# Attention by pairs of head pairs: shared rounds on TensorE, wider VectorE and ScalarE operations, later output statistics

## The chip, the cores and the metric

One core of a Trainium2 chip runs the whole program. The metric is the device time of one execution in microseconds. The tensors are float32 unless a line says otherwise.

## The reference

Two layers on 2048 tokens (8 sequences of 256) of width 256. Layer 0 is two mixtures of experts (stages A and B below), layer 1 is attention (C) and a mixture of 16 experts with two chosen per token (D):

```python
x = x + _L0_ffn_ref(_L0_cond_ref(x, cond_64, ...), ...)
x = x + _L1_ffn_ref(_L1_cond_ref(x, fside_16xSxS_0, mask_BxS_bk0, ...), ...)
```

The attention has 16 heads of 64, one shared key and value head, a null key and value, a bias per head (256 x 256), a mask per sequence, and a causal limit. Its input rows and its output rows are layer-normalized. The output feeds the routing of stage D.

## The kernel before

The program is written by hand: each engine has its own list of instructions, and semaphores join them. Stages A and B come first, then attention (`pe_attention`, `act_attention`, `dve_attention`, `pool_attention`, `sp_attention`), then D's expert matmuls. The change is in attention, some 275 us of the program.

Attention goes through 8 batches (sequences) b, and in each through 8 pairs of heads j; p = 8b + j numbers the 64 pairs. Every engine's loop has the same steps p, and works in each on different pairs:

- **GpSimd** (`pool_batch`): `pool_bm` makes the sum of mask and bias for pair p + 2, one instruction per head (L2306). Between these: the combination of stage B's results for the next batch (`pool_pairs`, L2320, L2324), the powers for both normalizations (`pool_row_rstd`, `pool_out_rstd`), the dispatch of routed rows (L2387, from batch 3 on), and in step 7 of batches 1 to 7, behind its second sum, a wait for `z_step`, after which `pool_z` and `pool_z_again` multiply and copy the last batch's output (L2366, L2374, L2375).
- **TensorE** (`pe_batch`): step p issues scores of pair p + 1 (`pe_scores`, two heads side by side in 64 rows each, L1609), the sums over values of pair p - 4 (`pe_sum`, 64 columns each, L1622), the queries of pair p + 3 (`pe_queries`, L1595) and the output products of pair p - 5 (`pe_out`, L1633). Beside them stand the turned rows, keys and values of the next batch (`pe_rows`, `pe_kv`, `pe_v_turn`) and the route of stage D for an earlier batch (`pe_z_turn`, `pe_z_logits`, `pe_z_counts`). Scores have two banks, by j: pair p waits until VectorE has read both heads of pair p - 2.
- **VectorE** (`dve_batch`): step p does, in this order, the block transpose of pair p's head 1 (`dve_blocks`, L2011), the scores of pair p + 1's head 1 (`dve_scores`, L1986: adds the mask sum and finds the row minimum), the output product with the reciprocals for pair p - 4 (`dve_o`, L2020), the block transpose of head 0, the reciprocals (L1993, L2000), in odd steps parts of the route search (`dve_dispatch`), and the scores of pair p + 1's head 0. `dve_scores_wait` waits for TensorE's scores and for both mask sums of the pair. Step 1 also has the statistics of the next batch's input, step 5 the raw output of the last batch (`dve_out_raw`, L2029), its statistics (L2033, L2038) and its variance (L2043).
- **ScalarE** (`act_batch`): step p does the exponentials of pair p + 1's two heads (`act_exp`, L1849, two pieces each), and between them the copy and scaling of the queries (`act_queries`, L1843) and in step 7 the normalization of the last batch's output (`act_out`, L1817), whose end is `z_step`.
- **SP's queue** (`sp_attention`): the transposed blocks of pair p are stored to DRAM (`sp_store_blocks`, L2484, 512 KB) and read back with partitions and rows exchanged (`sp_load_blocks`, L2495); the load of pair p - 1 is issued behind the store of pair p. Two block buffers stand in front of the stores, four behind the loads. Weights of stage D are loaded between them.

The head order is `ORDER = (1, 0)` and `LAG = 4`, so "first head" below is head 1.

## Time and profile before

| | us |
|---|---|
| median of 3 runs (781.17 to 783.06) | 781.69 |
| the profiled execution, its own time | 780.06 |
| its span, first to last instruction | 778.2 |
| busy in the span: TensorE / weight loads | 700.5 / 544.4 |
| busy: VectorE / ScalarE / GpSimd | 471.2 / 395.0 / 430.8 |

The granted clock of TensorE is 0.956 of full speed over the span, and 1.00 in the whole of attention. TensorE's busy time is modelled, because matmuls overlap; the start times of its instructions are not. Attention's first scores start at 361.3 us, its last output products at 635.7. A wait is put down to whatever ended last by the trace.

### The profile page before, as it was taken

How to read it: one execution, taken by the hardware profiler on the slowest of the kernel's cores; microseconds unless marked ns; L12 is line 12 of the kernel's file. 1: busy time of each engine (PE TensorE's matmuls, PEld its weight loads, DVE VectorE, ACT ScalarE, POOL GpSimd, SP SyncE). 2: the span in 40 equal slices, each digit the busy share in tenths (PEclk: the TensorE clock that was granted, in tenths of full speed). 3: DMA queues.
4: the chain of work that ended last, by engine and by line, in shares of the span. 5: the costliest groups of instructions: out<-in, count | busy, mean ns of one | idle time of the engine just before them, and what ended most of it. 6: DMA issues, size and time to landing. Idle time of an engine off the chain costs nothing. (4 is left out here: it accounts for less than half of the span.)

```text
span 778.2 us, 15602 instructions
## 1 busy us (share of the span) xinstructions
PE 700.5 (90%) x4389; PEld 544.4 (70%) x4390; DVE 471.2 (61%) x1730; ACT 395.0 (51%) x1100; POOL 430.8 (55%) x540
## 2 busy tenths in 40 slices
PE   8878998675899999998799999899999989998986
PEld 5457995455699999986566666566666654887865
DVE  1722457267444445424888888899998945354546
ACT  4444651124344444424767657576766625765611
POOL 1075604560555685243876877898896654255550
PEclk9897999795699999999999999999999999999999
DMA  9834534345377777541899999888888773455428
GB/s 324 315 95 117 156 106 132 102 132 207 103 228 228 219 219 203 158 148 58 305 312 343 317 351 327 297 295 270 306 266 298 267 282 106 123 148 151 132 80 320
DMA packets 120813, 166.22 MB, mean 214 GB/s; under 512 B 29984, under 2 KB 97056, under 8 KB 119840
## 3 DMA queue, kind: packets, MB, share of 16 engines
q1 hardware_dynamic: 103632, 127.65, 49.3%
q0 software_dynamic: 10944, 30.03, 12.5%
q10 hardware_dynamic: 6160, 7.64, 3.0%
q8 instruction: 34, 0.56, 0.3%
q14 instruction: 43, 0.35, 0.1%
HBM read 100.07 MB, written 65.21 MB: 212 GB/s over the span
## 5 line engine op out<-in xcount | busy, mean ns | idle before, releaser
L1849 ACT ACTIVATE work<-work 128x129 f32<-128x129 f32 (+1 forms) x256 | 114.4, 448 | 73.7 <-DVE work L1986 72.6
L2011 DVE STREAM_TRANSPOSE region_bd<-work 128x384 f32<-128x384 f32 x128 | 73.1, 571 | 13.4 <-DMA c_blocks<-region_bd 9.3
L1430 POOL DMA_INDIRECT d_pairs<-work,home x47 | 47.6, 1012 | 52.5 <-DVE home_f L1180 35.3
L1595 PE MATMUL psY<-work,region_ac 128*128 128x256 f32 x256 | 70.0, 396 | 3.8 <-ACT work L1843 3.8
L2306 POOL TENSOR_TENSOR work<-region_bd,region_ac 128x386 f32<-128x386 f32 x64 | 59.6, 939 | 19.1 <-DVE work L1986 11.1
L1419 POOL DMA_INDIRECT b_pairs<-work,home x39 | 38.1, 976 | 56.7 <-DVE work L1124 54.6
L2306 POOL TENSOR_TENSOR work<-work,region_ac 128x386 f32<-128x386 f32 x64 | 59.6, 943 | 17.3 <-DVE work L1986 9.3
L1411 POOL DMA_INDIRECT work<-in_x,inv x39 | 37.2, 953 | 56.0 <-DVE inv L1337 36.0
L1633 PE MATMUL psM<-region_ac,work 128*128 128x256 f32 x256 | 66.9, 384 | 0.0
L1082 ACT ACTIVATE work<-work 128x512 f32<-128x512 f32 x39 | 24.6, 630 | 80.5 <-issue 46.9
L1622 PE MATMUL psL<-region_bd,work 128*64 128x256 f32 (+1 forms) x512 | 55.8, 338 | 7.2 <-DVE work L2020 3.9
L902 PE MATMUL psH<-work,region_bd 128*128 128x128 f32 x472 | 59.6, 281 | 1.0 <-issue 1.0
L902 PEld LDWEIGHTS psH<-work,region_bd 128*128 128x128 f32 x472 | 57.0, 197 | 2.0 <-issue 1.9
L1622 PEld LDWEIGHTS psL<-region_bd,work 128*64 128x64 f32 x512 | 31.6, 136 | 38.4 <-issue 23.6
L1547 POOL DMA_INDIRECT work<-a_slots,slot_u x32 | 31.3, 978 | 45.8 <-DMA a_slots<-work 27.0
L1411 POOL DMA_INDIRECT work<-y_scratch,inv x39 | 37.7, 968 | 32.9 <-DVE inv L1337 21.3
L1595 PEld LDWEIGHTS psY<-work,region_ac 128*128 128x128 f32 x256 | 44.7, 189 | 14.0 <-ACT work L1843 5.7
L1633 PEld LDWEIGHTS psM<-region_ac,work 128*128 128x128 f32 x256 | 47.1, 190 | 8.5 <-issue 2.8
L1986 DVE CUSTOM_DVE_ANT_0 work<-psH,work 128x129 f32<-128x129 f32 (+1 forms) x128 | 39.6, 346 | 13.7 <-issue 8.6
L1849 ACT ACTIVATION_READ_ACCUMULATOR work<-work 128x1 f32 x256 | 47.9, 187 | 0.0
L963 PEld LDWEIGHTS psH<-work,acc 128*128 128x128 f32 x320 | 41.0, 201 | 0.9
L2387 POOL DMA_INDIRECT d_rows<-region_bd x32 | 32.2, 1008 | 16.2 <-DMA d_rows<-region_bd 6.9
(392 smaller groups left out, 1649.5 us busy)
## 6 DMA issues: line engine op xcount, KB each, us to landing
c_blocks<-region_bd SPq DMA_DIRECT2D x64, 512.0 KB
region_bd<-c_blocks SPq DMA_DIRECT2D x64, 512.0 KB
work<-d_rows SPq DMA_DIRECT2D x47, 132.0 KB
a_slots<-work SPq DMA_DIRECT2D x19, 256.0 KB
b_turned<-work SPq DMA_DIRECT2D x35, 128.0 KB
work<-b_turned SPq DMA_DIRECT2D x35, 128.0 KB
region_bd<-in_b_w SPq DMA_DIRECT2D x1, 3072.0 KB, 21.5
region_ac<-in_fside SPq DMA_DIRECT2D x12, 256.0 KB
```

Of the source, the lines that this page charges most:

```text
L902: last = pe.matmul(pair_h[p % DEEP][:, t % PAIR, j, :], f.w_in(j, k, t), xT[:, p % DEEP, t % PAIR, k, :], start=(k == 0), stop=(k == KD - 1))
L963: last = pe.matmul(ffn_h[u % RING][:, j * P:(j + 1) * P], f.w_in(j, k, u % RING), b_xT[:, u % RING, :, k, :], start=(k == 0), stop=(k == K ...
L1411: pool.indirect_dma_start(out=slot_rows(f, t), out_offset=None, in_=st.src, in_offset=bass.IndirectOffsetOnAxis(ap=inv[:, t:t + 1], axis=0 ...
L1419: pool.indirect_dma_start(out=st.pair_dram, out_offset=bass.IndirectOffsetOnAxis(ap=home[:, t:t + 1], axis=0), in_=ys[:, t % RING, :], in_ ...
L1430: pool.indirect_dma_start(out=st.pair_dram, out_offset=bass.IndirectOffsetOnAxis(ap=home[:, t:t + 1], axis=0), in_=d_ys[:, t % ROWS, :], i ...
L1595: last = pe.matmul(psY[:, 0:SEQ], c_wq[:, c, j * P:(j + 1) * P], c_xnT[:, odd, c, :], start=(c == 0), stop=(c == KD - 1))
L1622: last = pe.matmul(psL[DH * o:DH * o + DH, queries].rearrange("p (i a q) -> p i a q", a=4, q=32), c_v[:, b % 2, n, :], weights[:, o, block ...
L1633: last = pe.matmul(psM[:, i * DIM:(i + 1) * DIM], c_oT[:, p % 3, i * P:(i + 1) * P], c_wo[:, j, :], start=(j == 0 and i == 0), stop=(j == ...
L1849: nc.scalar.activation(c_p[:, j % 2, o, a:z], c_sc[:, o, a:z], ACT.Exp, scale=-1.0, bias=c_min[:, o, i:i + 1], accum_out=c_sum[:, j % 2, o ...
L1986: last = nc.vector.tensor_tensor_reduce(c_sc[:, o, a:z], psS[j % 2][:, o, a:z], c_bm[:, 2 * (j % 2) + o, a:z], 1.0, -LOWEST, ALU.add, ALU. ...
L2011: nc.vector.transpose(out=c_x1[:, p % 2, :, (QT + 1) * o:(QT + 1) * (o + 1), :].rearrange("p b i q -> p i b q"), in_=c_p[:, j % 2, o, 1:1 ...
L2306: pool.tensor_tensor(c_bm[:, 2 * (j % 2) + o, :], c_mp[b % 2], c_bias[:, 2 * j + o, :], ALU.subtract).then_inc(C.bm_ready, 1)
```

## The change

- **TensorE** works on two pairs at a time, in four groups a batch. The group of a = 8b + 2k issues the scores of pairs a + 2 and a + 3, the sums of a - 4 and a - 3, the queries of a + 4 and a + 5, and the output products of a - 6 and a - 5. In the third group (k = 2) the output products stand before the queries, else behind them. Two pairs' sums share one PSUM bank, and two pairs' queries another.
- **VectorE** makes the output product of two pairs in one instruction (512 columns) in even steps, for pairs p - 6 and p - 5, ahead of the scores. It no longer computes the two variances. The raw output stays in step 5 but moves behind the second head's scores, the statistics go to step 6 (the last batch: 7), and a part of the route search goes from step 5 to step 3.
- **ScalarE** scales two pairs' queries at once, at the start of even steps. The normalization `act_out` moves behind the second head's exponentials of step 7. Rows, keys and values of the next batch move ahead of a second head's exponentials.
- **GpSimd** adds the epsilon for both variances (two small instructions a batch), and `pool_out_rstd` stands between the two sums of step 7, not behind those of step 6.
- **Blocks**: four buffers in front of the stores instead of two; the new ones lie where experts 8 to 11 of `d_w13` go. The load of pair p - 2 is issued behind the store of pair p. Eight experts' weights are loaded in batch 1, and eight behind attention; before, it was twelve and four.

The core of the diff:

```diff
@@ pe_batch
-                if not (last and j == NPAIR - 1):
-                    pe_scores(pe, p + 1, (j + 1) % NPAIR, b + (j + 1) // NPAIR)
-                if s >= 0:
-                    pe_sum(pe, s, s % NPAIR, s // NPAIR)
...
+            for k in range(NPAIR // 2):
+                a = NPAIR * b + 2 * k
+                x = a - LAG
+                for p in (a + 2, a + 3):
+                    if p < pairs:
+                        pe_scores(pe, p, p % NPAIR, p // NPAIR)
+                for s in (x, x + 1):
+                    if s >= 0:
+                        pe_sum(pe, s, s % NPAIR, s // NPAIR)
+                if k == 2:
+                    pe_outs(pe, x - 2)
...
+                for p in (a + 4, a + 5):
+                    if p < pairs:
+                        pe_queries(pe, p, p % NPAIR, p // NPAIR % 2, p // NPAIR)
...
+                if k != 2:
+                    pe_outs(pe, x - 2)
@@ pe_attention, the end
-            for j in range(NPAIR - LAG, NPAIR):
-                pe_sum(pe, pairs - NPAIR + j, j, BATCH - 1)
-                pe_out(pe, pairs - NPAIR + j - 1, j - 1, BATCH - 1)
+            for j in range(NPAIR - LAG, NPAIR, 2):
+                for i in (j, j + 1):
+                    pe_sum(pe, first + i, i, BATCH - 1)
+                pe_outs(pe, first + j - 2)
...
-            pe_out(pe, pairs - 1, NPAIR - 1, BATCH - 1)
+            pe_outs(pe, first + NPAIR - 2)
@@ act_batch
                 if more:
                     act_exp(act, p + 1, j + 1, ORDER[0])
...
-                if not (last and j + 3 >= NPAIR):
-                    act_queries(act, p + 3, j + 3)
-                if j == 7 and not first and not last:
-                    act_out(act, b - 1)
...
                 if more:
                     act_exp(act, p + 1, j + 1, ORDER[1])
+                if j == 7 and not first and not last:
+                    act_out(act, b - 1)
@@ dve_blocks, dve_o
-            if p >= 2 and n == 0:
-                wait_dma(dve, C.blocks_stored, 0, p - 2)
+            if p >= 4 and n == 0:
+                wait_dma(dve, C.blocks_stored, 0, p - 4)
...
-            dve.wait_ge(C.pv_mm, p + 1)
+            dve.wait_ge(C.pv_mm, p + 2)
             wait_dma(dve, C.blocks_loaded, 0, p)
+            wait_dma(dve, C.blocks_loaded, 0, p + 1)
@@ dve_batch
                 dve_blocks(dve, p, j, ORDER[0])
                 if j == 0 and not first:
                     dve_v(dve, b)
+                if j % 2 == 0 and p >= LAG + 2:
+                    dve_o(dve, p - LAG - 2)
                 if more:
                     dve_scores_wait(dve, p + 1)
                     dve_scores(dve, p + 1, j + 1, ORDER[0])
-                if s >= 0:
-                    dve_o(dve, s, s % NPAIR)
...
-                if j == 5 and not first:
-                    dve_out_raw(dve, b - 1)
+                if j == 6 and not first and not last:
+                    dve_out_stats(dve, b - 1)
+                    dve.wait_ge(C.out_step, 4 * b - 2)
+                    dve_out_moments(dve, b - 1)
                 dve_dispatch(dve, b, j, last)
                 if more:
                     dve_scores(dve, p + 1, j + 1, ORDER[1])
...
+                if j == 5 and not first:
+                    dve_out_raw(dve, b - 1)
                     dve.wait_ge(C.out_raw, 2 * b)
@@ pool_batch
-                    if (j, n) == ((7, 0) if last else (6, 1)) and not first:
+                    if (j, n) == (7, 0) and not first:
                         pool_out_rstd(pool, b - 1)
@@ sp_attention
-            for p in range(pairs):
-                sp_store_blocks(sp, p)
-                if p >= 1:
-                    sp_load_blocks(sp, p - 1)
+            for a in range(0, pairs, 2):
+                for p in (a, a + 1):
+                    sp_store_blocks(sp, p)
+                    if a >= 2:
+                        sp_load_blocks(sp, p - 2)
```

How it moves instructions, at three places. **ScalarE, pair step 7 of a batch and the start of the next** (L1849 before and L1881 after are the exponentials, two pieces a head; L1843 and L1871 the queries; L1817 and L1840 the normalization). Before:

```order
L1849 ACTIVATE work<-work 128x129
L1849 ACTIVATE work<-work 128x257
L1843 ACTIVATE work<-psY 128x256
L1817 ACTIVATE acc<-acc,out_shift,out_rstd 128x256 x2
L1849 ACTIVATE work<-work 128x129
L1849 ACTIVATE work<-work 128x257
L1849 ACTIVATE work<-work 128x129
L1849 ACTIVATE work<-work 128x257
L1843 ACTIVATE work<-psY 128x256
```

After:

```order
L1881 ACTIVATE work<-work 128x129
L1881 ACTIVATE work<-work 128x257
L1881 ACTIVATE work<-work 128x129
L1881 ACTIVATE work<-work 128x257
L1840 ACTIVATE acc<-acc,out_shift,out_rstd 128x256 x2
L1871 ACTIVATE work<-psY 128x512
L1881 ACTIVATE work<-work 128x129
L1881 ACTIVATE work<-work 128x257
```

The normalization stood behind one head of its step and now stands behind both, with the double query operation behind it.

**TensorE, third group of a batch** (L1609 and L1614 are scores, L1622 and L1628 sums, L1633 and L1639 output products, L1595 and L1600 queries, L1650 and L1662 keys and values). Before, its step 5:

```order
L1609 MATMUL psH<-region_bd,work 128x129 x2
L1609 MATMUL psH<-region_bd,work 128x257 x2
L1622 MATMUL psL<-region_bd,work 64x256 x2
L1622 MATMUL psL<-region_bd,work 64x128 x2
L1650 MATMUL psX<-work,region_ac 128x256 x2
L1595 MATMUL psY<-work,region_ac 128x256 x2
L1609 MATMUL psHT<-region_bd,work 128x129 x2
L1609 MATMUL psHT<-region_bd,work 128x257 x2
```

After:

```order
L1639 MATMUL psM<-region_ac,work 128x256 x4
L1662 MATMUL psX<-work,region_ac 128x256 x2
L1614 MATMUL psH<-region_bd,work 128x129 x2
L1614 MATMUL psH<-region_bd,work 128x257 x2
L1614 MATMUL psHT<-region_bd,work 128x129 x2
L1614 MATMUL psHT<-region_bd,work 128x257 x2
L1628 MATMUL psL<-region_bd,work 64x2x128 x2
L1628 MATMUL psL<-region_bd,work 64x128 x2
L1628 MATMUL psL<-region_bd,work 64x2x128 x2
L1628 MATMUL psL<-region_bd,work 64x128 x2
L1639 MATMUL psM<-region_ac,work 128x256 x4
L1600 MATMUL psY<-work,region_ac 128x256 x4
```

Keys and values now end the group ahead, and the products that complete the last batch (first L1639 behind the sums) stand behind two pairs' scores and sums.

**GpSimd, pair step 7** (L2306 and L2328 are mask sums, L2366 and L2394 z). Before:

```order
L2348 TENSOR_TENSOR out_rstd<-out_rstd,minus_half 128x2
L2349 TENSOR_SCALAR out_shift<-out_mv 128x2
L2351 TENSOR_TENSOR out_shift<-out_shift,out_rstd 128x2
L2306 TENSOR_TENSOR work<-work,region_ac 128x386 x2
L2366 TENSOR_TENSOR region_bd<-acc,g_out 128x256 x2
```

After:

```order
L2328 TENSOR_TENSOR work<-region_bd,region_ac 128x386
L2374 TENSOR_SCALAR out_rstd<-out_mv 128x2
L2376 TENSOR_TENSOR out_rstd<-out_rstd,minus_half 128x2
L2377 TENSOR_SCALAR out_shift<-out_mv 128x2
L2379 TENSOR_TENSOR out_shift<-out_shift,out_rstd 128x2
L2328 TENSOR_TENSOR work<-region_bd,region_ac 128x386
L2394 TENSOR_TENSOR region_bd<-acc,g_out 128x256 x2
```

The powers moved between the two sums of step 7 and gained the addition in front; z still stands behind the second sum.

## Rows read from the trace of the kernel before

**Rows 1.** Busy time by stretch: batches 1 and 5
```profile
core 0: us, PE busy (x) PEld busy (x) DVE busy (x) ACT busy (x) POOL busy (x), PEclk, DMA share, GB/s
...
389.50:420.00 30.50, 30.23 (x203) 20.90 (x202) 26.01 (x118) 20.64 (x79) 21.38 (x30) 1.00 0.95 324
...
522.20:555.30 33.10, 31.84 (x220) 22.42 (x219) 30.56 (x143) 22.60 (x85) 29.14 (x41) 1.00 0.84 287
```

**Rows 2.** Timeline of VectorE at the scores of a batch's third pair
```profile
start us, us, engine line op out<-in xcount [idle before <-releaser]
532.88 0.29 DVE L1986 CUSTOM_DVE_ANT_0 work<-psH,work 128x129 f32<-128x129 f32 x1 [1.26 <-POOL work L2306]
...
565.98 0.29 DVE L1986 CUSTOM_DVE_ANT_0 work<-psH,work 128x129 f32<-128x129 f32 x1 [1.24 <-POOL work L2306]
```

**Rows 3.** Timeline of GpSimd from z to the third pair's sums
```profile
527.35 1.42 POOL L2366 TENSOR_TENSOR region_bd<-acc,g_out 128x256 f32<-128x256 f32 x2 [2.25 <-ACT acc L1817]
...
531.88 0.87 POOL L2306 TENSOR_TENSOR work<-region_bd,region_ac 128x386 f32<-128x386 f32 x1
```

**Rows 4.** Timeline of ScalarE in pair step 7 of batch 4
```profile
526.19 1.08 ACT L1817 ACTIVATE acc<-acc,out_shift,out_rstd 128x256 f32<-128x256 f32 x2
527.82 0.40 ACT L1849 ACTIVATE work<-work 128x129 f32<-128x129 f32 x1 [0.54 <-DVE work L1986]
...
528.62 0.19 ACT L1849 ACTIVATION_READ_ACCUMULATOR work<-work 128x1 f32 x1
```

**Rows 5.** Timeline of TensorE, two pairs, and a wait for a load
```profile
481.98 0.93 PE L1609 MATMUL psHT<-region_bd,work 64*128 64x129 f32 x8
482.84 0.87 PE L1622 MATMUL psL<-region_bd,work 128*64 128x256 f32 x8
483.64 1.13 PE L1633 MATMUL psM<-region_ac,work 128*128 128x256 f32 x4
484.61 1.03 PE L1595 MATMUL psY<-work,region_ac 128*128 128x256 f32 x4
485.47 1.03 PE L1633 MATMUL psM<-region_ac,work 128*128 128x256 f32 x4
486.43 0.93 PE L1609 MATMUL psH<-region_bd,work 64*128 64x129 f32 x8
489.13 0.87 PE L1622 MATMUL psL<-region_bd,work 128*64 128x256 f32 x8 [1.77 <-DMA region_bd<-c_blocks]
```

**Rows 6.** Timeline of VectorE in batch 5: product, variances, step, search
```profile
533.44 0.42 DVE L2020 TENSOR_TENSOR work<-psL,region_bd 128x256 f32<-128x256 f32 x1
533.78 0.57 DVE L2011 STREAM_TRANSPOSE region_bd<-work 128x384 f32<-128x384 f32 x1
...
537.05 0.36 DVE L1963 TENSOR_SCALAR in_rstd<-in_mv 128x2 f32<-128x2 f32 x1
537.32 0.57 DVE L2011 STREAM_TRANSPOSE region_bd<-work 128x384 f32<-128x384 f32 x1
...
540.30 0.57 DVE L2011 STREAM_TRANSPOSE region_bd<-work 128x384 f32<-128x384 f32 x1
...
551.39 0.19 DVE L2085 TENSOR_REDUCE region_bd<-psH 128x2 f32<-128x32 f32 x1
...
551.96 0.28 DVE L1986 CUSTOM_DVE_ANT_0 work<-psH,work 128x129 f32<-128x129 f32 x1
...
553.58 0.52 DVE L2043 TENSOR_SCALAR out_rstd<-out_mv 128x2 f32<-128x2 f32 x1
```

**Rows 7.** Waits of VectorE: for a block store; for the route counts, last batch
```profile
486.54 0.58 DVE L2011 STREAM_TRANSPOSE region_bd<-work 128x384 f32<-128x384 f32 x1 [1.30 <-DMA c_blocks<-region_bd]
...
DVE region_bd L2106 <- PE psH L1696: 1.4, 1, 1.4
```

**Rows 8.** Chain that ended last: last output products; first expert matmuls
```profile
634.15 1.92 PE psM L1633 x8
...
663.04 1.78 PE psH L902 x16
```

209 lines of the change are left out of this document (108 added, 101 removed).

## The prediction

> **What bounds the kernel now.** I read the attention stage batch by batch first (busy time per stretch), then VectorE's waits in the timeline, then what stands on the other engines just before each wait. By the first view TensorE seems to be the bound: in batch 1 it is busy 30.23 of 30.50 us, in batch 5 31.84 of 33.10 [rows 1]. But its busy time is modelled, and VectorE has 30.56 of 33.10 in batch 5 as the sum of its instructions. The timeline decides. Once a batch, at the scores of its third pair, VectorE stands still: 1.26 us before 532.88, 1.24 before 565.98, and what came last was a bias-and-mask sum of GpSimd [rows 2]. Between those two points its timeline has no gap over 0.25 us. So the period of a batch, here 33.10 us, is a loop: a chain that starts at GpSimd's late sum, runs through a full VectorE, and comes back to GpSimd.
>
> The way back: behind the second sum of pair step 7 GpSimd waits until ScalarE has normalized the last batch's output (two ACTIVATEs, 1.08 us from 526.19), and starts at 527.35 after 2.25 us idle; z, its copies and the next two sums follow in its order, so the second sum (531.88, 0.87 us) ends at 532.75 and VectorE goes on at 532.88 [rows 2, 3, 4]. From the end of the normalization to VectorE's restart this is 5.6 us, fixed. In steps 1 to 7 VectorE then works without a break until the scores that ScalarE's next normalization stands behind. TensorE is beside this loop, not in it, from batch 2 on. Only in batches 0 and 1, which have no route search on VectorE, does it set the pace.
>
> **TensorE: pairs by twos.** Before, each pair walks through scores, sums, and 128-row products. Starts are 481.98, 482.84, 483.64, 484.61, 485.47, 486.43: scores take 0.86, sums 0.80, products behind sums 0.97, products between products 0.86, products ahead of scores 0.96 [rows 5]. The scores stream 386 columns for two heads side by side where a product streams 512 in 0.86, so 0.65 of their 0.86 is streaming; for the sums' 384 it is 0.64 of 0.80. With 0.11 and 0.10 around the products, a round has 0.58 us of changes between array shapes. Two pairs now share one round: 0.29 us a pair, 2.3 a batch. The products, loads and queries themselves are as many as before. In batch 1 this is path, but the DMA engines are busy 0.95 there [rows 1], which leaves some 1.5 us: I take 2.2 (ends 1.5 and 2.8), and 1.3 for batch 0, where steps of VectorE wait for sums that now come later (ends 0 and 2.6). In batches 2 to 7 the 2.3 us lie beside VectorE's loop and give nothing.
>
> Here the Trainium skill speaks against the change: "Perfetto Trace Analysis", Identifying the Most-Contended Engine, wants the engine with the highest occupancy improved first and does not trust matmul busy time, but the share of weight loads. By that share TensorE is at 22.42 of 33.10 in batch 5, so by the rule the 2.3 us are worth nothing there; by matmul busy time the sum would be 12 us lower. The gaps of VectorE agree with the rule.
>
> **VectorE.** Output products for two pairs are one instruction of 512 columns instead of two of 256. One holds VectorE for 0.34 us, from 533.44 to 533.78 [rows 6]; for 512 columns the ends are 0.61 (only 256 further columns at the slope of this row) and 0.68; I take 0.64, 0.04 less for two, 0.1 in steps 1 to 6. Both variances go to GpSimd: 0.27 (537.05 to 537.32) and some 0.43 (0.52 by its row at 553.58) [rows 6]. With four block buffers a transpose waits for the store four pairs back, not two: three such waits stand in batches 2 and 3, 3.3 us together (one, of 1.30, is shown [rows 7]); they go. In sum VectorE's part of the loop shrinks by 0.8 us a batch, and by small gaps of 0.3.
>
> **ScalarE: the normalization moves.** In step 7 it stood between the exponentials of the first and the second head; now it stands behind the second. Before, it started at 526.19 and the second head's exponentials ran from 527.82 to 528.81 [rows 4]. They start 0.34 earlier now, since step 7 has no output product, and so the normalization starts near 528.5: 2.3 us later. GpSimd waits these 2.3 us, its sums for the third pair come 2.3 later, and VectorE, which already waits there, waits for them in full. The earlier statistics cover nothing: out_rstd was ready early, and also a pair later it is ready before 528.5. Moved queries, rows and key copies on ScalarE fall into its idle time (busy 22.60 of 33.10 [rows 1]); the double query op of the first step stands behind the normalization, but its scores are wanted some 4 us after it, and VectorE is then still waiting for GpSimd. GpSimd's two small additions (0.2 each by its similar ops) are in its 2.25 us of idle time. So far the loop is 2.3 - 0.8 - 0.3 = 1.2 us longer.
>
> **A new wait: the raw output of step 5.** The products of the previous batch's last two pairs stand in the third double group of TensorE, behind scores that wait until VectorE has ended step 4. From there: scores 0.86, two sums 1.44, four products 1.83, together 4.1 us. VectorE's step 5 is shorter: a whole step with an output product is 2.98 (537.32 to 540.30), without it 2.64, and half of the route search adds 0.57 (551.39 to 551.96) [rows 6], so it is at the raw output after 3.2 us and waits 0.9. Since the group ahead also carries turned rows and keys and values, TensorE can be 0.1 to 0.6 late: 0.9 to 1.5, and I take 1.2, and nothing of it can be hidden, because VectorE has no other work in front. Before, one pair's products stood in time. Steps 5 to 7, the normalization and GpSimd all follow: the loop is 2.4 us longer than before.
>
> **DMA.** Loads of odd pairs are issued a pair later than they were, while the sums are wanted one pair later only for even pairs; so an odd pair loses up to one step of its room. In the trace of before a load holds the sums up seldom, at most by 1.77 us [rows 5]; outside batch 1 TensorE has the room to take such a wait. I price it at nothing, and its other end is rival (c). Four experts' weights (1 MB) leave batch 2, and 2 MB plus the bias stand at the end: about 4 MB, at the 324 GB/s of batch 1 [rows 1] some 13 us from the last products at 634.15; the first expert matmul is at 663.04 [rows 8], so they stay hidden; 0.3 for the crowd.
>
> **The sum**, against the profiled execution (span 778.2 us, its own time 780.06; the median of the runs is 781.69, 1.6 above it):
> - batches 0 and 1: -2.2 - 1.3, and the normalization later by 1.5 (2.3, less a route search of 0.8 that step 7 doesn't have yet): -2.0
> - five loops from the third pair of batch 2 to that of batch 7: 5 x 2.4 = 12.0, less 0.7 (one store wait, batch 2) and 2.2 (two of 1.3, of which I give 0.4 back to loads in a crowded queue, batch 3): +9.1
> - last batch: -1.4 for a wait on the counts (1.4 us, once [rows 7]), which are made a group earlier now, -1.3 for step 7 without output product and the smaller VectorE sum, and +1.7, because the four products of pairs 60 and 61 now stand behind the sum of pair 63, which waits for the last load; before, only two pairs' products (1.92 [rows 8]) did: -1.0
> - weights: +0.3
>
> Together +6.4: 786.5 for the profiled execution, **788.1 us** for the median.
>
> **Rivals.**
> (a) *The loop does not bind.* If the later normalization is absorbed, because the way from it to the third pair's sums gets shorter or z is not what GpSimd waits for, VectorE loses its wait (1.25) and keeps its own saving (0.8): 31.0 us a batch, into which TensorE fits with 31.8 - 2.3 = 29.5. Six batches at -2.1 and -2 in front: 767. For it: TensorE's 96%, the removal of 0.58 us per round. Against it: VectorE waits for GpSimd at the third pair of batches 2 to 6, and reaches it without a gap in batch 7. It decides where VectorE's wait at the third pair gets to zero: 1.25 and 2.3, some 3.5 us, would have to go. The Trainium skill's "TensorEngine Tiling (Array Packing)", Key Properties, says that a change of tiling mode drains TensorE, by which the saving on TensorE itself is real; rows 5 agree with 0.10 before each change. Chance 0.24.
> (b) *Only the normalization costs.* TensorE gets to the products of step 5 in time (scores of the group not held until step 4 ends): 1.2 less in five loops, 782. For it: room on TensorE. Against: the double scores. Chance 0.18.
> (c) *Loads too late.* Odd pairs' sums wait 1 us in the nine or so groups where DMA is over 0.95 busy, and VectorE with them: 797. Chance 0.08.
> Forecast as above: 0.50, its own range 784 to 793.
>
> **Numbers.** 0.3% is 2.3 us, about what a measurement of this kernel can tell: faster is below 779.3, slower above 784.0. (a) is all faster, (b) nearly all the same, forecast and (c) slower: 0.25, 0.18, 0.57. The range takes in the nearer half of (a) and most of (c): 772 to 795.
>
> **What would show it.** Right: VectorE waits for GpSimd at the third pair of batches 2 to 7 for some 3.5 us, not 1.3; the normalization starts after the second head's exponentials; a wait of about 1 us in front of the raw output of step 5; batch period near 35.5; TensorE busy near 29.5 a batch, with rounds of 6.6 us for two pairs. Wrong: periods of 31 to 32, or waits at the third pair under 1 us; then (a) holds. If instead TensorE's sums wait for DMA, it is (c).

## The result, and the profile after

The changed kernel takes **803.35 us** (median of 4 runs, 802.45 to 804.17); the kernel before took 782.0 beside it. The ratio is **1.027** (95% interval 1.0254 to 1.029). The forecast was 788.1 with a range up to 795: the direction holds, the size does not. In the profiled executions the difference is 24.1 us (spans of 802.4 and 778.2). It divides as follows, at marks taken from VectorE's first scores of a pair and from the first expert matmul:

| from, to | before | changed | difference | forecast |
|---|---|---|---|---|
| start to scores of pair 0 | 362.4 | 360.8 | -1.6 | 0 |
| pair 0 to pair 18 (third of batch 2) | 68.2 | 69.2 | +1.0 | -2.0 |
| pair 18 to pair 58, five loops | 166.7 | 186.3 | +19.5 | +9.1 |
| pair 58 to pair 63 | 21.6 | 23.3 | +1.7 | } -0.7 in all |
| pair 63 to the first expert matmul | 44.0 | 47.4 | +3.4 | } |
| rest | 115.4 | 115.4 | 0.0 | 0 |

The loop of a batch, first. VectorE's timeline at the third pairs of batches 5 and 6, answering to [rows 2], and then its waits from the one to the other (waiter, what it waited for: us in total, times, longest):

```profile
start us, us, engine line op out<-in xcount [idle before <-releaser]
542.49 0.29 DVE L2014 CUSTOM_DVE_ANT_0 work<-psH,work 128x129 f32<-128x129 f32 x1 [3.72 <-POOL work L2328]
...
579.96 0.29 DVE L2014 CUSTOM_DVE_ANT_0 work<-psH,work 128x129 f32<-128x129 f32 x1 [3.72 <-POOL work L2328]
```

The waits:

```profile
DVE work L2014 <- POOL work L2328: 3.7, 1, 3.7
DVE work L2014 <- PE psH L1614: 1.2, 1, 1.2
DVE acc L2058 <- PE psM L1639: 1.2, 1, 1.2
DVE region_bd L2039 <- ACT work L1881: 0.6, 1, 0.6
```

Two of the four were forecast: 3.7 at the third pair and 1.2 in front of the raw output. Two were not: 1.2 at the scores of the pair four behind the third (pair 46 here; the texts below write 8b+14, with b one batch back), which is where TensorE's scores (L1614) come late, and 0.6 at a transpose, behind ScalarE. The loop is 37.5 us instead of 33.1. The way back on ScalarE, from its timeline, answering to [rows 4]:

```profile
573.20 1.07 ACT L1840 ACTIVATE acc<-acc,out_shift,out_rstd 128x256 f32<-128x256 f32 x2
```

And on GpSimd, answering to [rows 3]:

```profile
574.35 1.42 POOL L2394 TENSOR_TENSOR region_bd<-acc,g_out 128x256 f32<-128x256 f32 x2 [3.52 <-ACT acc L1840]
```

From the start of the normalization to the next third pair it is 6.8 us (573.20 to 579.96), as before (526.19 to 532.88, 6.7). All of the loss lies in the other part, from the third pair to the normalization: 26.3 us before (499.89 to 526.19), 30.7 now (542.49 to 573.20). The row of the kernel before at which this part starts:

```profile
499.89 0.29 DVE L1986 CUSTOM_DVE_ANT_0 work<-psH,work 128x129 f32<-128x129 f32 x1 [1.41 <-issue]
```

What the two unexpected waits are, TensorE's timeline shows:

```profile
549.81 1.23 PE L1614 MATMUL psHT<-region_bd,work 64*128 64x129 f32 x8 [1.99 <-DVE work L2014]
550.97 2.83 PE L1628 MATMUL psL<-region_bd,work 128*64 128x256 f32 x16
...
558.64 0.93 PE L1614 MATMUL psH<-region_bd,work 64*128 64x129 f32 x8
```

And the busy time by stretch of the same batch, with the granted clock as PEclk:

```profile
core 0: us, PE busy (x) PEld busy (x) DVE busy (x) ACT busy (x) POOL busy (x), PEclk, DMA share, GB/s
542.50:550.30 7.80, 4.79 (x33) 3.71 (x33) 7.59 (x37) 4.51 (x17) 7.39 (x12) 1.00 0.47 153
550.40:553.70 3.30, 3.30 (x20) 1.67 (x16) 3.03 (x16) 2.15 (x8) 3.30 (x5) 0.50 1.00 313
553.80:580.00 26.20, 23.63 (x170) 18.35 (x171) 18.97 (x86) 15.51 (x56) 19.16 (x28) 1.00 0.84 274
```

Just behind the third pair TensorE is busy only 4.79 of 7.80 us, with one idle stretch of 1.99, and then its granted clock stands at 0.50, the lower of its two levels (1.2 GHz), for 3.3 us. Two pairs' sums take 2.83 there, against 1.45 in the chain below. From 549.81 on TensorE has no further gap, and it reaches the scores that VectorE then waits 1.2 us for only at 558.64. In the kernel before the clock was at 1.00 through the whole attention [rows 1]. In this trace such a fall begins 4 to 8 us behind the third pair of each of the batches 2 to 6, that is, in each of the five loops. This is the first theory: **the longer wait at the third pair leaves TensorE idle, its clock falls, and the slow matmuls make VectorE wait again.**

The end, from the chain that ended last (start, us, what), answering to [rows 8]:

```profile
644.52 5.78 DMA region_bd<-c_blocks
650.30 0.04 issue
650.34 0.87 PE psL L1628 x8
651.21 1.93 PE psM L1639 x8
653.14 1.72 PE psY L725 x4
654.85 1.45 PE psL L1628 x16
656.30 3.65 PE psM L1639 x16
```

### The profile page after: what moved, and what is told of

Its sections match the earlier page's. It is cut to its first block and busy times, and to the rows that moved or that the text cites. A ratio compares the mean times of both kernels' runs of the same rounds, so it can differ in the third digit from the quotient of the medians.

```text
span 802.4 us, 15513 instructions
## 1 busy us (share of the span) xinstructions
PE 693.1 (86%) x4389; PEld 551.9 (69%) x4390; DVE 466.1 (58%) x1682; ACT 391.2 (49%) x1069; POOL 437.1 (54%) x556
## 5 line engine op out<-in xcount | busy, mean ns | idle before, releaser
L1881 ACT ACTIVATE work<-work 128x129 f32<-128x129 f32 (+1 forms) x256 | 114.2, 448 | 76.8 <-DVE work L2014 75.4
L2328 POOL TENSOR_TENSOR work<-region_bd,region_ac 128x386 f32<-128x386 f32 x128 | 118.6, 937 | 37.1 <-DVE work L2014 26.7
L1600 PE MATMUL psY<-work,region_ac 128*128 128x256 f32 x256 | 63.4, 391 | 0.0
L1639 PE MATMUL psM<-region_ac,work 128*128 128x256 f32 x256 | 61.2, 383 | 0.0
L1628 PE MATMUL psL<-region_bd,work 128*64 128x256 f32 (+1 forms) x512 | 57.5, 371 | 3.9 <-DMA region_bd<-c_blocks 3.9
L2014 DVE CUSTOM_DVE_ANT_0 work<-psH,work 128x129 f32<-128x129 f32 (+1 forms) x128 | 39.7, 347 | 35.7 <-POOL work L2328 20.6
L1628 PEld LDWEIGHTS psL<-region_bd,work 128*64 128x64 f32 x512 | 35.7, 153 | 30.5 <-issue 17.9
L1416 POOL DMA_INDIRECT work<-y_scratch,inv x39 | 37.7, 965 | 33.2 <-DVE inv L1342 21.6
L1639 PEld LDWEIGHTS psM<-region_ac,work 128*128 128x128 f32 x256 | 47.9, 190 | 8.3 <-issue 2.2
L1600 PEld LDWEIGHTS psY<-work,region_ac 128*128 128x128 f32 x256 | 47.7, 194 | 8.1 <-issue 1.9
L1614 PE MATMUL psHT<-region_bd,work 64*128 64x129 f32 (+1 forms) x256 | 31.3, 362 | 22.1 <-DVE work L2014 21.9
L1881 ACT ACTIVATION_READ_ACCUMULATOR work<-work 128x1 f32 x256 | 48.0, 187 | 0.0
L1614 PE MATMUL psH<-region_bd,work 64*128 64x129 f32 (+1 forms) x256 | 31.0, 362 | 11.9 <-ACT work L1871 10.2
L2415 POOL DMA_INDIRECT d_rows<-region_bd x32 | 32.2, 1007 | 15.9 <-DMA d_rows<-region_bd 7.0
```

What stands on the lines that cost most here:

```text
L1416: pool.indirect_dma_start(out=slot_rows(f, t), out_offset=None, in_=st.src, in_offset=bass.IndirectOffsetOnAxis(ap=inv[:, t:t + 1], axis=0 ...
L1600: last = pe.matmul(psY[:, (k % 2) * SEQ:(k % 2 + 1) * SEQ], c_wq[:, c, j * P:(j + 1) * P], c_xnT[:, odd, c, :], start=(c == 0), stop=(c == ...
L1614: last = pe.matmul(psS[j % 2][:, o, a:z], c_qr[half, j % 2, i * P:(i + 1) * P], c_kT[half, i:i + z - a], start=True, stop=True)
L1628: last = pe.matmul(sums[DH * o:DH * o + DH, queries, :, :], c_v[:, b % 2, n, :], weights[:, o, blocks, :, :], start=(n == 0), stop=(n == 1))
L1639: last = pe.matmul(psM[:, i * DIM:(i + 1) * DIM], c_oT[:, p // 2 % 2, i, p % 2, :], c_wo[:, j, :], start=(j == 0 and i == 0), stop=(j == N ...
L1881: nc.scalar.activation(c_p[:, j % 2, o, a:z], c_sc[:, o, a:z], ACT.Exp, scale=-1.0, bias=c_min[:, o, i:i + 1], accum_out=c_sum[:, j % 2, o ...
```

## Experiments

Chips differ: the kernel before takes 782 to 788 us on one sort and 740 to 742 on the other, where the stages ahead of the attention are 28 us shorter. The five loops of attention are not shorter: two of the versions below, the same up to its last transfers, take 161.1 us for them on the faster chip and 160.9 on the slower. (Batches 0 and 1 are less steady: 69.1 and 66.0 us in the same two traces.) So totals are given as ratios to the kernel before on the same chip, and loops in us, from third pair to third pair, batch 2 to batch 7.

### The normalization back between the heads

```
                 if j == 5 and not first and not last:
                     act_keys(act, b + 1)
                     act_values(act, b + 1)
+                if j == 7 and not first and not last:
+                    act_out(act, b - 1)
                 if more:
                     act_exp(act, p + 1, j + 1, ORDER[1])
-                if j == 7 and not first and not last:
-                    act_out(act, b - 1)
```

> The changed kernel (803.35 us) with the two normalization ACTIVATEs of step 7 put back between the exponentials of the first and of the second head; all else as changed. They can then start at about 570.7 instead of 573.2 in batch 5, so VectorE's wait at the third pair falls from 3.7 by about 2.6 to about 1.1 us. Theory (the long wait idles TensorE, its granted clock falls to 0.5 once a batch, and the slow matmuls cost VectorE another 1.9 us a batch): the clock stays at 1.0 in most or all batches, the waits at the scores of pair 8b+14 (1.2) and at the transposes (0.6 to 1.0) go too, period 37.5 -> 33 to 33.5, total 803 - 5.5 x 4.2 = 780 us. Rival 1 (those 1.9 us belong to the double groups themselves, the clock is a by-product): period 35 or so, total 789. Rival 2 (GpSimd waits for something else than the normalization): unchanged, 803.

Ratio **1.009** (1.0065 to 1.0122). The loops are 34.78, 33.46, 34.80, 33.45, 34.80. VectorE's wait for GpSimd at the third pair is gone from batch 3 on (2.00 are left in batch 2, where the first loop starts); what it waits for there now is TensorE's scores, 0.6 or 1.2 us. Its waits in the fourth loop, of 33.45 us, with those at both its ends:

```profile
DVE work L2014 <- PE psH L1614: 1.2, 3, 0.6
DVE acc L2058 <- PE psM L1639: 1.2, 1, 1.2
DVE work L2014 <- PE psHT L1614: 1.2, 1, 1.2
```

Busy time by stretch, fourth and fifth loop:

```profile
502.60:536.00 33.40, 30.83 (x235) 23.96 (x233) 29.59 (x136) 22.86 (x80) 28.49 (x41) 1.00 0.83 281
536.00:570.80 34.80, 31.59 (x213) 24.25 (x211) 29.78 (x136) 22.39 (x80) 28.59 (x39) 0.90 0.79 260
```

The loops with the clock at 1.00 are the shorter ones, and the others are 1.35 us longer. So the normalization is the largest single cause, but the clock can still fall without the long wait (here some 24 us behind the third pair, in every other loop, each time for 6.8 us). The expectation was met in half: the theory had 33 to 33.5 with the clock up in most batches and 780 us; the ratio means 789, the number of its rival 1, because three of the five loops have a fall. VectorE's instructions take 29.6 us a loop, 1.0 less than in [rows 1].

### Only the normalization moved, in the kernel before

```
-                if j == 7 and not first and not last:
-                    act_out(act, b - 1)
                 if j == 6 and last:
                     act_shared_halves(act, 1, 2)
                 if more:
                     act_exp(act, p + 1, j + 1, ORDER[1])
+                if j == 7 and not first and not last:
+                    act_out(act, b - 1)
```

> The kernel before (782 us) with only the normalization of step 7 moved behind the second head's exponentials. Priced from its own rows at 2.3 to 2.6 us a batch in five loops. If the loop is all there is: VectorE's wait at the third pair 1.25 -> 3.6 to 3.8, clock at 1.0, 782 + 5 x 2.5 = 794.5. If a third-pair wait of that size lets TensorE's clock fall also here, where TensorE has 2.3 us a batch more to do: 794.5 + up to 5 x 1.9 = 796 to 804. If the loop does not bind here: 782.

Ratio **1.019** (1.0169 to 1.0214), 14.4 us, and the loops 36.41, 37.98, 36.19, 36.26, 35.72: 15.8 us more than before in five. VectorE's row at the third pair:

```profile
550.79 0.29 DVE L1986 CUSTOM_DVE_ANT_0 work<-psH,work 128x129 f32<-128x129 f32 x1 [3.88 <-POOL work L2306]
```

The wait grew by 2.6 (from 1.26 [rows 2]), the distance by which the two ACTIVATEs moved (526.19 to the end of the second head's exponentials at 528.81). The loop there (36.26) is 3.2 longer than a clean one before (33.1): 2.6 for the wait, 0.3 for a wait for a store, 0.3 of small ones. The clock falls in four of the five loops, where it never fell before, but the one without a fall (36.41, where the kernel before has 33.38) lost 3.0, about as much as the others, so in this kernel, with single groups on TensorE, the clock's own part is small. The falls begin 0.5 to 2.6 us behind the third pair here; why they cost less is not shown. One moved pair of instructions is thus two thirds of what the whole change costs.

### The raw output a step later

```
                 dve_recs(dve, p)
+                if j == 6 and not first:
+                    dve_out_raw(dve, b - 1)
+                    dve.wait_ge(C.out_raw, 2 * b)
                 if j == 6 and not first and not last:
                     dve_out_stats(dve, b - 1)
...
-                if j == 5 and not first:
-                    dve_out_raw(dve, b - 1)
-                    dve.wait_ge(C.out_raw, 2 * b)
```

> The changed kernel with VectorE's raw output (two adds) moved from the end of pair step 5 to behind the reciprocal transposes of step 6, where the statistics stand. Theory (VectorE waits 1.2 us a batch for the products of the previous batch's last two pairs, and has a step of other work to put in front): the 1.2 us go from 6 batches, period 37.5 -> 36.3, total 796 us. Rival (TensorE's next double group, whose products need the bank read, then waits instead and passes it on; or the third-pair wait grows by the same, since the statistics and the normalization come as late as before): 801 to 804.

Ratio **1.024** (1.0217 to 1.0264). Loops: 34.37, 34.59, 34.47, then 36.48 and 35.49. The wait at the raw output is gone from each. Windows of the third and fourth:

```profile
475.70:510.20 34.50, 32.25 (x237) 25.13 (x234) 29.54 (x136) 22.29 (x80) 30.08 (x43) 1.00 0.85 288
510.20:546.70 36.50, 32.90 (x221) 24.63 (x220) 29.69 (x137) 22.16 (x80) 30.03 (x43) 0.91 0.80 260
```

Same program, same work, 2.0 us apart. In the fourth the clock falls 4.5 us behind the third pair, and VectorE waits 1.2 at the scores and 0.9 at a transpose; in the third it does not fall, and there is one wait of 0.35. The ratio is nearer to the rival's 801 to 804 than to the theory's 796, but not for the rival's reason: the wait at the third pair did not grow (2.15 to 3.73). Batch 0 of this trace is 5 us longer than in the others, which the record leaves open.

### The output products first, on TensorE

```
+                if k == 2:
+                    pe_outs(pe, x - 2)
                 for p in (a + 2, a + 3):
                     if p < pairs:
                         pe_scores(pe, p, p % NPAIR, p // NPAIR)
```
(and removed behind the sums.)

> The changed kernel with only the output products of the third double group put in front of its scores; the normalization stays late. Theory: the 1.2 us at the raw output go from the loop as they did when the raw output was moved a step later (ratio 1.024 then, loops of 34.4 to 34.6 without and 36.5 with a clock fall), so the ratio is again 1.020 to 1.025 and the loops are 34.5 or 36.4. Rival: the scores come late instead, loops of 37 to 38, ratio 1.027 or more.

> The changed kernel with the normalization back between the heads and, on TensorE, the four output products of the third double group in front of its scores instead of behind its sums; VectorE's order as changed. Theory: VectorE's wait of 1.2 us at the raw output goes, since the products no longer stand behind scores that wait for step 4; TensorE does them in its idle time. Loops without a clock fall 33.45 -> 32.2 to 32.6, total 738 to 743 us, ratio 0.995 to 1.001. Rival (the scores behind the products now come late by 1.8 us, and VectorE waits there instead): loops of 33.4 to 34, ratio 1.009 to 1.015.

Ratios 1.032 (1.0265 to 1.0373) and 1.011 (1.0061 to 1.0156): the rival in both, with loops of 37.65 to 37.93 (the fifth 36.21) and 34.21 (the first 35.06). The wait at the raw output goes, and the scores behind the products come late. VectorE's timeline in the first of the two kernels:

```profile
496.29 0.29 DVE L2014 CUSTOM_DVE_ANT_0 work<-psH,work 128x129 f32<-128x129 f32 x1 [2.97 <-PE psH L1614]
```

So that wait can be taken away on VectorE (by work put in front of it), not by the order on TensorE.

### Is it the clock?

A first filler, constant transposes on TensorE in its idle places near the third pair:

> The changed kernel with 128-column transposes of a constant (0.11 us each, results unused) on TensorE where it stands idle around the third pair of a batch: 5 before and 4 behind the expert logits of the first double group, 14 in front of the second scores of the second double group. The normalization stays late. Theory (clock): the granted clock stays at 1.0 through the attention, VectorE's waits at the scores of pair 8b+14 (1.2) and at the transposes (0.6 to 1.0) vanish, the one at the third pair stays at 3.5 to 3.7, period 37.5 -> about 35.6, total 803 - 5.5 x 1.9 = 793 us. Rival 1 (double groups themselves cost the 1.9): clock at 1.0 but no gain, 803 or up to 2 us more from the filler. Rival 2 (the fall has another cause than idling, so the clock still falls): 803 to 806.

Ratio 1.027 (1.0239 to 1.0294), undecided: loops of 37.36, 38.40, 36.68, 35.88, 35.36. No fall lies near a third pair, yet in the first, third and fifth loop VectorE waits 1.24 at the scores of the fourth pair behind it all the same, with the clock at 1.00: the filler delayed the scores itself. In batch 2 VectorE had freed the bank at 409.96, and the 14 transposes held the second scores back until 411.83. In three of the loops the clock fell 25 to 28 us behind the third pair. So the changed kernel was traced again, once on the faster chip and once beside a better filler.

> The changed kernel itself once more, for a trace and a ratio from the same chip as the experiments (there the kernel before took 742 us; the stages ahead of the attention were 28 us shorter). The attention should be as in its first trace: third-pair periods of 37.3 to 37.8 us with one fall of TensorE's clock in each, 18th to 58th pair 186 us, ratio 1.027, about 762 us. If the clock falls differently here, loops without a fall should take 35.5.

> The changed kernel a third time, to stand beside the next run on the same chip. Its loops have so far taken 35.6 to 36.0 us when TensorE's clock did not fall within 4 to 8 us behind the third pair, and 37.3 to 37.8 when it did. Here each loop should be one of the two, by where its fall lies; ratio to before 1.027 to 1.030.

Ratios 1.0295 (1.0248 to 1.0341) and 1.032 (1.0269 to 1.0368). In the first of the two traces the loops are 35.65, 35.85, 35.79, 35.86 and 36.00, with a fall 24 to 26 us behind the third pair in the first four. In the second they alternate: 35.63, 37.49, 35.72, 37.32, 35.98 (the fifth loop is some 1.5 us shorter by itself; in the kernel before it takes 31.35). VectorE's waits in its third loop, apart from those at the third pair and the raw output:

```profile
DVE region_bd L2039 <- ACT work L1881: 0.7, 1, 0.7
DVE work L2014 <- PE psH L1614: 0.3, 1, 0.3
```

The same in its fourth loop:

```profile
DVE region_bd L2039 <- ACT work L1881: 1.3, 2, 0.8
DVE work L2014 <- PE psH L1614: 1.2, 1, 1.2
```

And the stretches at the falls in these two loops:

```profile
475.10:500.70 25.60, 22.60 (x164) 17.56 (x162) 23.38 (x109) 17.32 (x62) 23.75 (x34) 1.00 0.81 276
500.90:504.10 3.20, 3.20 (x20) 2.10 (x17) 3.06 (x15) 1.62 (x9) 0.64 (x1) 0.50 0.90 304
504.30:517.70 13.40, 12.01 (x88) 9.82 (x87) 9.61 (x46) 7.08 (x25) 11.94 (x18) 1.00 0.62 197
517.90:521.10 3.20, 2.97 (x18) 1.96 (x20) 3.00 (x16) 2.85 (x10) 3.20 (x5) 0.50 0.85 272
```

Where the fall lies decides. At 500.90 it is close ahead of the normalization: what it delays comes mostly behind it, and VectorE waits at the next third pair anyway (there 2.83 instead of 3.7, so the loss is taken out of that wait). At 517.90, 7 us behind the third pair at 510.80, all of it is on VectorE's way to the normalization, and the loop pays in full. The traces of the raw output later (34.4 to 34.6 and 36.5) and of the kernel with the last load moved (35.64 without a fall, 37.28, 37.34, 37.50 with one 7 us behind the third pair) show the same step. Over the four traces of the changed kernel's attention, this one among them, 13 of 20 loops have a fall within 9 us behind the third pair. They take 37.3 to 37.8 us, or 36.0 to 36.3 where it is the fifth; the seven others take 35.6 to 35.9. With the normalization back there is no wait for GpSimd at the third pair that a late fall could come out of, and there it costs 1.35. In batch 1, ahead of the five loops, the same wait of 1.2 at the scores stands in each trace of the changed kernel without a fall near the third pair; there it is not the clock's.

The better filler: besides the 5 + 4 around the expert logits, in both places where TensorE idles, from batch 3 on only.

```
+                    if k == 1 and b >= 3 and p == a + 3:
+                        pe_keep_clock(pe, psY, 14)
+                    if k == 3 and b >= 3 and not last and p == a + 3:
+                        pe_keep_clock(pe, psY, 14)
                     if p < pairs:
                         pe_scores(pe, p, p % NPAIR, p // NPAIR)
```

> The changed kernel with constant transposes on TensorE (0.11 us each) in the idle places of the second double group (5 + 4 around the expert logits, 14 in front of the second scores) and of the fourth (14 in front of the second scores), from batch 3 on only. The normalization stays late and VectorE's wait at the third pair stays 3.5 to 3.7. Theory (the late normalization costs what its own wait says, and all beyond 35.5 us a loop is the clock): no fall of the clock near the third pair, the four loops from the third pair of batch 3 on take 35.3 to 35.8 us with waits of under 0.4 at the scores of pair 8b+14, where the changed kernel has 37.3 to 37.8 when its clock falls there. Rival (the waits at the scores come from the double groups themselves): loops of 37 and more with the clock up. In total the filler saves 0 to 7 us against the changed kernel beside it, by how its falls lie.

Ratio **1.022** (1.0173 to 1.0265) where the changed kernel beside it had 1.032: the medians are 7.9 us apart, for work that computes nothing. One stretch over all five loops:

```profile
402.10:580.20 178.10, 170.10 (x1264) 132.90 (x1261) 147.87 (x677) 111.95 (x400) 142.97 (x202) 1.00 0.83 276
```

VectorE's waits in the fourth loop, with the third-pair waits at both its ends:

```profile
DVE work L2021 <- POOL work L2335: 7.5, 2, 3.7
DVE acc L2065 <- PE psM L1639: 1.2, 1, 1.2
DVE work L2021 <- PE psH L1614: 0.3, 1, 0.3
```

The clock is at 1.00 throughout, the third-pair wait is still 3.7, the wait at the scores is 0.3, and all the loops are 35.65, 35.88, 36.37, 35.90, 34.37. The loops are up to 0.6 above the expected 35.3 to 35.8; in 36.37 the filler itself made the scores 0.97 late. With the two fillers there are nine loops with transposes in front of the second scores, and none has a fall near the third pair, against 13 of 20 without. (The first loop of this run has none there and stayed clean by chance.) Against 37.3, 37.5, 37.8, 37.5, 36.3 of the first trace, the loops are 1.4 to 1.9 us shorter each, 8.1 in all; the rival (double groups as such) is out.

The 7.9 us between the medians are not all these loops'. Between the two profiled executions of this pair, 10.9 us apart, the five loops make 4.0 (182.1 against 178.2, since two loops beside it were clean too). Pair 58 to 63 makes 1.9, where a fall is gone as well. Another 3.9 lie between pair 63 and the first expert matmul, where no filler stands; their cause is not shown.

### Both put back, and the end

The normalization between the heads and the raw output in step 6, together:

> The changed kernel with both: the normalization back between the two heads' exponentials and the raw output a step later. Additive theory: a loop of the changed kernel is 34.4 + 1.2 (raw output behind the products) + 1.9 (clock fall) = 37.5, and 2.1 of it is the late normalization. Then loops without a fall take 33.45 - 1.2 = 32.2 us and with one 33.6; against 33.0 to 33.4 of the kernel before, total 0.992 to 1.0 of before, 737 to 742 us. Rival 1 (with the raw output at step 6 the statistics come too late for the early normalization, which then waits for GpSimd's reciprocal root): ScalarE stands before the second head's exponentials, loops of 33.5 to 34.5, ratio 1.005 to 1.015. Rival 2 (TensorE sets the pace as soon as the third-pair wait is gone): loops of 33.4, ratio 1.009 as with the normalization alone.

Ratio **0.995** (0.9914 to 0.9978): loops of 33.37, 32.82, 32.18, 32.11, 30.63 (and 33.33, 32.62, 32.19, 32.13, 30.63 in the trace of the same version with a load moved, below), close to the additive theory's 32.2, or 33.6 with a fall. That is 0.5% faster than the kernel before, and the kernel before measured against itself gave 1.004 (below), so the total alone is little to go by; but the three versions with both put back all lie below 1, on three chips, and the five loops take 161.1, 160.9 and 165.4 us in their traces, against 166.3 and 166.7 in the two of the kernel before. For the end, the load of pair 61 was moved ahead of the store of pair 63, in the changed kernel and in this one, and then one shared-expert product was moved on TensorE (and its reader on ScalarE):

```
-                    if a >= 2:
+                    if a >= 2 and (a < pairs - 2 or p == a):
                         sp_load_blocks(sp, p - 2)
+                    if a == pairs - 2 and p == a:
+                        sp_load_blocks(sp, p - 1)
...
-                if j == NPAIR - LAG:
-                    pe_shared_halves(pe, 3, 4)
...
             pe_z_turn(pe, BATCH - 2)
-            pe_shared_halves(pe, 4, 5)
+            pe_shared_halves(pe, 3, 4)
             pe_z_logits(pe, BATCH - 2, psX)
-            pe_shared_halves(pe, 5, 6)
+            pe_shared_halves(pe, 4, 6)
```

> The changed kernel (1.0295 of before) with one transfer moved: at the end, the load of pair 61's blocks is issued in front of the store of pair 63 instead of behind it. Theory: the sums of pair 61 wait 2.3 us for that load, and 9.6 us of TensorE's fixed work follow; the load is issued some 2.5 us earlier and the wait goes, then the load of 62 or VectorE's products set the start of the rest: -1.5 to -2.3 us, 761 us, ratio 1.0265. Rival (store 63 and the loads 62 and 63 behind it come late instead, since the moved load takes the DMA engines first): 763 to 764.

> The changed kernel with the normalization between the heads, the raw output a step later, and the last load of pair 61 earlier. The first two alone gave 0.9946 of before (0.9914 to 0.9978), loops of 32.1 us without a clock fall. If the tail's wait of 0.85 to 2.3 us goes, 737.5 to 739 us, ratio 0.991 to 0.994; if it is only moved to the later loads, 0.9946 again.

> The version with the normalization between the heads, the raw output a step later and the earlier load of pair 61 (0.9935 of before, 0.9914 to 0.9956), with one shared-expert product moved on TensorE and ScalarE from between the last sums to behind the turn of batch 6's rows. Theory (behind the last load TensorE runs a fixed chain, and this product of 1.72 us is in it, while 1.57 us of idle time stand before the turn of batch 7's rows): from the last pair's scores to the first expert product 48.1 -> 46.5 to 47.3 us, ratio 0.992. Rival (the last load sets the end of the sums, or the moved product delays the second turn): 48 us, ratio 0.9935.

Ratios 1.027 (1.0224 to 1.0307), 0.9935 (0.9914 to 0.9956) and 0.994 (0.9913 to 0.9967): the three intervals overlap those of the same kernels without the step, so neither step is shown to gain or to cost. In its trace the moved load gains nothing (pair 63 to the first expert matmul 48.0 instead of 47.4): the store of pair 63 then takes 8.2 us instead of 4.9. The moved product shows 46.6 instead of 48.1, in an execution of 741.8 us where the median is 737.0, so no more is read from it. There the chain that ended last runs through the last store and load:

```profile
593.91 6.15 DMA c_blocks<-region_bd
600.08 3.61 DMA region_bd<-c_blocks
603.69 0.04 issue
603.73 0.87 PE psL L1628 x8
604.60 3.65 PE psM L1639 x16
```

Of the 3.4 us lost at the end, 1.73 are the double products (3.65 against 1.92 [rows 8]). The rest shifts between TensorE's fixed chain and the last transfers; which of the two holds it in the changed kernel was not separated, and neither was the part of the 2 MB of weights that now stand behind attention. The better kernel has loops of 32.2 with the clock at 1.00; its fourth, by stretch:

```profile
526.30:558.50 32.20, 30.12 (x227) 23.39 (x223) 29.61 (x137) 22.66 (x80) 30.12 (x43) 1.00 0.88 296
```

VectorE's waits there, with those at both ends of the loop:

```profile
DVE work L2014 <- PE psHT L1614: 2.5, 2, 1.3
DVE work L2014 <- PE psH L1614: 0.3, 1, 0.3
```

All of them are for TensorE's scores, with the clock up: in this kernel TensorE is in the loop, and VectorE's wait at the third pair is for TensorE instead of GpSimd.

The kernel before, traced again on the slower chip, for the marks:

> The kernel before once more, for a trace from this chip. If the two chips differ only ahead of and behind the attention, its third-pair periods are again 33.0 to 33.4 (one of 35.9), 18th to 58th pair 167 us, first expert matmul 302 us after the first scores; then the changed kernel's 21 us are: about 1.5 up to the 18th pair, 12.4 in the five loops (179.1, its trace on this chip), 1.7 to the last pair and 3.3 behind it.

Ratio 1.004 (1.0004 to 1.0072) for the unchanged kernel. Loops of 33.58, 35.33, 32.96, 33.07, 31.34 and no fall of the clock in attention: as in its first trace.

## Why the prediction was wrong in size

**Right.** The bound is a loop through GpSimd's sum, VectorE, ScalarE's normalization and back; putting the normalization back removed VectorE's wait for GpSimd at the third pair from batch 3 on, and moving it alone made the kernel before slower. Wait at the third pair 3.7 (forecast 3.5), raw output 1.2 (about 1, in the sum 1.2), VectorE's instructions 0.8 to 0.9 less a loop (29.80, and 29.68 in a clean loop, against 30.56), all as worked out. A loop without a fall near its third pair takes 35.6 to 35.9; the forecast was "near 35.5". TensorE's busy time near 29.5 a batch shows only where the long wait is gone (30.12 in the better kernel; 31.9 in the changed one, with a part at half clock). Rounds of two pairs take 6.7 us (558.64 to 566.06, less 0.74 of waiting; forecast 6.6). No rival came: VectorE waits for GpSimd at the third pair of batches 2 to 7 (a), 1.2 at the raw output in each loop (b), and in the loops it waits for no load or store (c). That of the raw output's wait "nothing of it can be hidden" held for VectorE's order as it was, but the two adds could move.

**The step that failed** is "TensorE is beside this loop, not in it", and with it "outside batch 1 TensorE has the room". It was beside the loop only while its clock stayed up. The forecast added the wait at the third pair to GpSimd's side and did not ask what TensorE does in the meantime. It idled there (busy 4.79 of 7.80 us), its clock went to 0.50, and VectorE then waited for its scores. The forecast had no term for this. It is 8.1 to 8.8 of the 17.7 us by which the profiled execution missed the forecast: 186.3 for five loops in the first trace against 178.2 with the filler, or 177.5 for the best clean ones (the four of the second trace and the 34.37 of the filler). Even with the clock up TensorE is not beside the loop once the wait for GpSimd is gone: what VectorE then waits for is its scores, up to 1.3 us at the third pair.

The rest of the 17.7 us, with 8.8 for the clock: 1.7 in clean loops, 3.0 in batches 0 and 1, 6.1 in the last batch and at the end; the start (-1.6) and the weights (-0.3) go the other way.

**Terms of the sum that were mis-sized.**
- Five clean loops: 177.5 - 166.7 = +10.8, forecast +9.1. From the third on, a clean loop is 2.8 to 3.0 longer where 2.4 was forecast. Measured in a clean one (35.90 against 33.10): the wait at the third pair grew by 2.5 where the later normalization was put at 2.3 (2.6 less 0.34 for an earlier start), the raw output is 1.2 as forecast, and VectorE's instructions are 0.9 less. The 0.3 for small gaps did not come. That makes 2.8. The slope by which 512 columns were to hold VectorE 0.61 to 0.68 us is not in the row that it names; the next instruction starts 0.57 us behind it, so the pair saves 0.1, not 0.04.
- Batches 0 and 1: forecast -2.0, measured +1.0. From the first scores to the third pair of batch 1 the changed kernel is 2.0 shorter, 1.3 of it behind the third pair of batch 0, where -1.3 was forecast. In batch 1 it is 3.0 longer (35.73 against 32.70), where -0.7 was forecast. The period scatters between traces: 34.3 to 36.1 in four of the changed kernel, 32.7 and 33.3 in two of the kernel before. With the normalization back it is 32.80, with both back 32.0 to 33.2. So of the 2.2 forecast for TensorE's rounds 0.7 shows there (32.01 against 32.70, the best of each), and the late normalization costs some 2.5 (35.4, the mean of four, against 32.80) where 1.5 was forecast. The raw output waits 2.1 in this batch and had no term; how much of it would be hidden otherwise was not separated.
- The last batch: forecast -1.0, measured +5.1. The raw output waits 2.8 there and was not in that term at all. With it a step later pair 58 to 63 takes 19.7 instead of 23.3, or 20.9 to 21.5 where the normalization is back too; with the filler, which takes away a fall in this batch, the wait is 1.1 and the stretch 21.7. So raw output and clock share this loss. The end costs 3.4 instead of 1.7.

The medians are 21.4 us apart where the profiled executions are 24.1: the profiled one of the kernel before is 1.9 below its median (780.06 against 782.0), and that of the changed kernel 0.8 above. In which stretch the others differ is not on record.

## What to carry to other kernels

When a change lets the critical engine wait longer, ask what an engine beside the loop does meanwhile: if TensorE idles, its clock may fall, and it comes back at half speed when it is wanted. Saving work on an engine that does not bind may so cost time, which these runs suggest and do not prove: with the normalization back the clock fell in three of five loops where the kernel before has none, but the kernel before with the late normalization has falls too, with no work saved. In the changed kernel a slowdown counted in full on the part of the loop ahead of the instruction that closes it; a slowdown close to that instruction disappeared in the wait behind it. And before the order on an engine is changed to cure a wait, look at who stands behind the moved work: the products moved on TensorE gave a wait of 2.97 for one of 1.2, the adds moved on VectorE cost nothing.

## What the runs showed of the hardware

- The same program can fall or not fall at the same place: in three traces of the changed kernel TensorE was idle for 1.99, 1.82 and 1.88 us before the second scores of the second double group. At the first two its clock went to 0.50, at the third it stayed at 1.00 and fell some 20 us later. Loops of one execution alternate between 35.7 and 37.4 us, with the fall near the third pair in the long ones.
- With constant transposes (14 of 0.11 us) in two idle places a batch the clock was at 1.00 through 178 us, with VectorE's wait at the third pair still 3.7. In nine loops with transposes in front of the second scores no fall came near the third pair, against 13 of 20 without. Where they found no idle time they held the scores up (1.2 us in three loops, 0.97 in one).
- With one load at the end issued 2 us earlier, the store behind it took 8.2 us instead of 4.9, and the sums came no sooner (one trace each).
